# A group of low probabilities and half of h's low parts moved to GpSimd, odd heads' keys to ScalarE, one gate operation fewer

## The chip, the cores and the metric

The kernel runs on one core of a Trainium2 chip. The metric is the device time of one execution in microseconds, the median of several runs. An execution was also recorded by the hardware profiler; its rows are quoted below. Engines are named as the profile names them: PE is TensorE's matrix products and PEld its weight loads, DVE is VectorE, ACT is ScalarE, POOL is GpSimd, SP is the engine that issues the transfers.

## The reference

One gated block works on 32 rows of a batch. x has 256 tokens of 256 numbers in each row, the context y has 77 tokens of 192 numbers. There are 16 heads of 16 numbers, and 8 experts of which the best two count.

```python
# attention of the image tokens to the context, then a two-layer MLP
q, k, v = x_normed @ Wq + bq, y @ Wk + bk, y @ Wv + bv      # 16 heads of 16
attn = softmax(q k^T * scale)
h = relu((attn v) @ W1 + b1)
x = x + tanh(g_xattn) * (h @ W2 + b2)
# gated experts on the normed result
scores = maximum(x_normed2 @ gate_W + gate_b, 1e-4)
p = softmax(scores); keep the top 2, w = maximum(p, 0.1) over their sum
x = x + tanh(g_ffn) * sum_e w_e (x_normed2 @ expert_W[e] + expert_b[e]) / 2
```

## The kernel before

**High and low parts.** To keep fp32 accuracy with faster matrix products, most operands are split: a rounded high part (fp16 or fp32r) and a low part, which is the value less its high part. A product is then three products (low with high, high with low, high with high). ScalarE usually makes the high part out of PSUM, and VectorE or GpSimd the low part by a subtraction.

**Steps.** `run` calls `step(pair, u, s)` on every engine for s from 0 to 34. One step works on four rows of the batch at once, each at another stage: row b = s is in front (norm, keys, values, queries, row maxima), row m = s - 1 is in the middle (attention, MLP, second norm), row e = s - 2 is first with the experts (gate, products 0 to 4), and row f = s - 3 is last (products 5 to 7, store). Each engine has its own program, and the order of the calls in its `step` is the order of its work. Engines wait for each other by counting semaphores only. TensorE's order in a step is in `step` at line 965, VectorE's at 1354, ScalarE's at 641, GpSimd's at 446.

**Attention.** A row has eight groups of two heads. `exps` (ScalarE, L557 and L558) makes the exponentials of a group twice, as f32 `p_f` and as rounded `p_hi`; `p_low` makes `p_lo` as their difference on GpSimd (L373) or VectorE (L1182). `POOL_LOW` and `VECTOR_LOW` say which groups are whose: before, GpSimd has 1, 3, 4, 5, 6 and VectorE 0, 2, 7. `attend` on TensorE waits for the group's low part. The buffers hold four groups.

**The MLP.** `mlp_up` puts h into PSUM in two halves; `relus` (ScalarE, L603) writes each of four quarters twice, high part `h_hi` and f32 `h_f`; `h_low` (VectorE, L1277) subtracts them to `h_lo`; `mlp_down` (TensorE, L918) uses the quarters c = 0 to 3 in turn, with h's parts as weights that are loaded, and waits for the low part of each quarter the first time it needs it. `add_mlp` and the second norm follow on VectorE, with the scale of the norm on GpSimd (`second_norm_scale`), then `second_norm_transposes` on TensorE.

**Keys.** Sixteen stacked key blocks are transposed into one PSUM bank, `T_KEYS`. `kz_copy` copies the even heads' half on ScalarE (L611) and the odd heads' half on VectorE (L1252). The second half of the second MLP layer writes the same bank and waits for both copies.

**The gate.** Thirteen small operations on VectorE (`gate`, L1308), each behind the one before by the semaphore `gate_op`: scores with bias (`graw`), their maximum with 1e-4 (`gs`, L1323), the largest (`gm1`), the shifted scores (`gshift`) that ScalarE's `gate_exps` waits for (L639), differences of all pairs (`gdiff`, L1330), comparisons (`gbeat`, L1333), counts, sums, weights, `comb`. `stack_comb` on GpSimd waits for the last one.

**GpSimd's order in a step** is the low probabilities of row m, then key blocks (L427) of row b around `stack_comb`, the keys' low part, three additions for the experts' result, the queries' low part (L385), the values' two parts (L419, L421), the first norm's scale, the residual with its bias (`x_with_bias`, L366), and the second norm's scale (L358, L361).

## Time and profile before

| | |
|---|---|
| median of 3 runs | 1005.38 us |
| the runs | 1005.3, 1008.52, 1005.38 us |
| the profiled execution | 1003.91 us, span 1002.2 us |
| granted TensorE clock over the span | 0.977 of full speed |
| VectorE busy | 834.1 us in 2137 instructions |
| ScalarE busy | 732.1 us in 1517 instructions |
| GpSimd busy | 650.5 us in 856 instructions |

The span is the time from the first to the last instruction of the profiled execution. Matrix products are pipelined and their ends are modelled, so a following product can start before the one in front is shown as ended. A row of a timeline gives the start in us from the span's start, the length in us, the engine, the line of the kernel, the operation, what it writes and reads, and how many equal ones are merged; in brackets stands the idle time of the engine just before, and what ended it.

### The profile page before, as it was taken

How to read it: one execution, taken by the hardware profiler on the slowest of the kernel's cores; microseconds unless marked ns; L12 is line 12 of the kernel's file. 1: busy time of each engine (PE TensorE's matmuls, PEld its weight loads, DVE VectorE, ACT ScalarE, POOL GpSimd, SP SyncE). 2: the span in 40 equal slices, each digit the busy share in tenths (PEclk: the TensorE clock that was granted, in tenths of full speed). 3: DMA queues.
4: the chain of work that ended last, by engine and by line, in shares of the span. 5: the costliest groups of instructions: out<-in, count | busy, mean ns of one | idle time of the engine just before them, and what ended most of it. 6: DMA issues, size and time to landing. Idle time of an engine off the chain costs nothing.

```text
span 1002.2 us, 26189 instructions
## 1 busy us (share of the span) xinstructions
PE 941.7 (94%) x9410; PEld 668.3 (67%) x9410; DVE 834.1 (83%) x2137; ACT 732.1 (73%) x1517; POOL 650.5 (65%) x856
## 2 busy tenths in 40 slices
PE   3669999999999999999999999999999999999997
PEld 2446766766766776776777676677667766776753
DVE  5777888888888888888888889888888888888875
ACT  4756878777787877778787777778777877877661
POOL 5435766667776666776666677666677766666743
PEclk8589999999999999999999999999999999999999
DMA  6000000000000000000000000000000000000000
GB/s 196 27 14 11 15 14 25 25 25 22 26 14 15 25 26 25 23 23 17 15 25 25 25 23 14 26 15 25 25 25 22 15 17 23 25 12 12 12 13 22
DMA packets 17473, 24.62 MB, mean 25 GB/s; under 512 B 2799, under 2 KB 8897, under 8 KB 17345
## 3 DMA queue, kind: packets, MB, share of 16 engines
q1 hardware_dynamic: 17344, 22.94, 7.3%
q8 instruction: 77, 1.26, 0.5%
q14 instruction: 52, 0.42, 0.1%
HBM read 14.54 MB, written 8.39 MB: 23 GB/s over the span
## 4 chain that ended last, share of the span: by engine, by line
PE 56%; POOL 16%; DVE 9%; issue 9%; ACT 7%; DMA 1%; SPq 1%; POOLq 0%; DVEq 0%; ACTq 0%
PE e L735 19%; PE g L735 11%; PE t L918 9%; POOL k_block L427 8%; POOL p_lo L373 6%; PE t L784 4%; ACT p_hi L558 2%; PE g L935 2%; DVE stats L1086 2%; PE s L869 2%; DVE acc L1199 2%; PE s L804 1%; DVE kz L1252 1%; PE g L744 1%; DVE p_lo L1182 1%
## 5 line engine op out<-in xcount | busy, mean ns | idle before, releaser
L373 POOL TENSOR_TENSOR p_lo<-p_f,p_hi 77x512 f16<-77x512 f32 x160 | 183.4, 1162 | 227.6 <-ACT p_hi L558 227.6
L735 PE MATMUL e<-we_hi,x2T_lo 128*128 128x512 f16 x496 | 189.7, 382 | 4.8 <-DVE acc L1199 4.8
L735 PE MATMUL e<-we_hi,x2T_hi 128*128 128x512 f16 x496 | 188.9, 381 | 0.0
L735 PE MATMUL e<-we_lo,x2T_hi 128*128 128x512 f16 x496 | 188.9, 381 | 0.0
L557 ACT ACTIVATE p_f<-t 77x512 f32<-77x512 f32 x256 | 154.3, 603 | 24.2 <-PE t L784 23.8
L1199 DVE SCALAR_TENSOR_TENSOR acc<-e,comb,acc 128x256 f32<-128x256 f32 x307 | 146.0, 475 | 13.5 <-PE e L735 11.1
L558 ACT ACTIVATE p_hi<-t 77x512 f16<-77x512 f32 x256 | 154.4, 603 | 0.0
L1244 DVE TENSOR_REDUCE row_max<-s 128x6 f32<-128x462 f32 (+1 forms) x192 | 108.3, 578 | 32.1 <-PE s L869 32.0
L804 PEld LDWEIGHTS s<-v_hi,p_lo 77*128 77x128 f16 x1024 | 83.4, 96 | 38.3 <-issue 22.2
L804 PE MATMUL s<-v_hi,p_lo 77*128 77x17 f16 x1024 | 97.9, 172 | 11.0 <-DVE p_lo L1182 4.1
L806 PE MATMUL s<-v_hi,p_hi 77*128 77x17 f16 x1024 | 96.4, 170 | 0.0
L805 PE MATMUL s<-v_lo,p_hi 77*128 77x17 f16 x1024 | 96.3, 171 | 0.0
L427 POOL TENSOR_TENSOR k_block<-own_head,khT 128x616 f16<-128x616 f16 x64 | 93.6, 1464 | 4.1 <-ACT khT L588 4.1
L784 PE MATMUL t<-qsT,kz 128*77 128x256 f16 x512 | 90.6, 279 | 2.6 <-ACT p_hi L558 2.4
L735 PEld LDWEIGHTS e<-we_hi,x2T_hi 128*128 128x128 f16 x496 | 48.6, 98 | 59.2 <-issue 1.1
L603 ACT ACTIVATE h_hi<-g,b_cols,w_unscale 128x256 fp32r<-128x256 f32 x128 | 73.3, 572 | 19.8 <-PE g L735 19.8
L805 PEld LDWEIGHTS s<-v_lo,p_hi 77*128 77x128 f16 x1024 | 82.5, 97 | 7.3 <-issue 0.3
L806 PEld LDWEIGHTS s<-v_hi,p_hi 77*128 77x128 f16 x1024 | 81.6, 96 | 0.0
L615 ACT ACTIVATE qsT<-g 128x1024 f16<-128x1024 f16 x32 | 32.7, 1023 | 66.2 <-PE g L935 66.2
L735 PEld LDWEIGHTS e<-we_hi,x2T_lo 128*128 128x128 f16 x496 | 48.3, 97 | 48.1 <-DVE acc L1199 12.2
L1182 DVE TENSOR_TENSOR p_lo<-p_f,p_hi 77x512 f16<-77x512 f32 x96 | 73.7, 768 | 7.9 <-ACT p_hi L558 3.7
L918 PE MATMUL t<-w_hi,h_lo 128*128 128x256 f32 x256 | 77.3, 302 | 2.0 <-DVE h_lo L1277 1.4
(193 smaller groups left out, 2900.3 us busy)
## 6 DMA issues: line engine op xcount, KB each, us to landing
x_sb<-in_x SPq DMA_DIRECT2D x32, 256.0 KB, 2.6
out<-acc SPq DMA_DIRECT2D x32, 256.0 KB, 2.0
we_f<-in_L_ffn_expert_W SPq DMA_DIRECT2D x2, 1024.0 KB, 11.0
y_sb<-in_ctx SPq DMA_DIRECT2D x32, 57.8 KB
w_f<-in_L_xattn_W SPq DMA_DIRECT2D x2, 512.0 KB, 7.3
wq_f<-in_L_xattn_Wq SPq DMA_DIRECT2D x1, 256.0 KB, 3.9
wkv_f<-in_L_xattn_Wk SPq DMA_DIRECT2D x1, 192.0 KB, 3.1
wkv_f<-in_L_xattn_Wv SPq DMA_DIRECT2D x1, 192.0 KB, 3.9
```

Of the source, the lines that this page charges most:

```text
L373: pool.tensor_tensor(p_lo[:, r].rearrange("m h n -> m (h n)"), p_f[:, r, :], p_hi[:, r].rearrange("m h n -> m (h n)"), ALU.subtract).then_ ...
L427: pool.tensor_tensor(k_block[:, c * PAIRS:(c + 1) * PAIRS, :], own_head[:], khT[:, c, :].unsqueeze(1).to_broadcast([P, PAIRS, M]), ALU.mul ...
L557: act.activation(p_f[:, r, :], TT[g % 2][0:M, :], ACT.Exp, scale=SCALE).then_inc(exps_done, 1)
L558: act.activation(p_hi[:, r].rearrange("m h n -> m (h n)"), TT[g % 2][0:M, :], ACT.Exp, scale=SCALE).then_inc(exps_done, 1)
L735: mm = pe.matmul(out_ap, a, c, start=(i == 0), stop=(i == n - 1))
L784: mm = pe.matmul(TT[g % 2][0:M, e * N:(e + 1) * N], kz[:, g, e, :], qsT[:, g, :], start=True, stop=True)
L804: pe.matmul(dst, lo, v_hi[:, u, h, :], start=True, stop=False)
L805: pe.matmul(dst, hi, v_lo[:, u, h, :], start=False, stop=False)
L806: mm = pe.matmul(dst, hi, v_hi[:, u, h, :], start=False, stop=True)
L918: mm = pe.matmul(T_DOWN[t][:, 0:D], a[:, c, rows], w[:, c, :], start=(c == 0 and i == 0), stop=(c == HC - 1 and i == 2))
L1199: dve.scalar_tensor_tensor(out=acc[:, u, t, :], in0=BANK[product_banks(r)[i]][:, j * D:(j + 1) * D], scalar=comb[:, u, t, 2 * c + j:2 * c ...
L1244: dve.tensor_reduce(row_max[:, t, h:h + n], S[i % 2][:, 0:n * M].rearrange("p (h m) -> p h m", h=n), AX.X, ALU.max).then_inc(max_taken, 1)
```

## The change

- `POOL_LOW` is (1, 2, 3, 4, 5, 6) and `VECTOR_LOW` (0, 7): group 2's low probabilities are made by GpSimd.
- `h_low` of quarters 1 and 3 runs on GpSimd, quarters 0 and 2 stay on VectorE. The semaphore `h_lo_done` becomes two, `h_lo_vector` and `h_lo_pool`. On GpSimd quarter 1 stands behind `q_low` and ahead of `v_parts`, quarter 3 behind `v_parts`.
- `kz_copy` on VectorE is gone; ScalarE copies both halves, one behind the other.
- The gate has 12 operations. `graw` has a ninth column that holds 1e-4, so the largest can be taken of the raw scores, and the maximum with 1e-4 is made together with the subtraction of the largest. The comparisons use the shifted scores. One more memset fills the ninth column once.
- On GpSimd `x_with_bias` moves behind the second norm's scale.

```diff
-CONSTS = EARLY + 1 + 7
+CONSTS = EARLY + 1 + 8
-POOL_LOW = (1, 3, 4, 5, 6)
-VECTOR_LOW = (0, 2, 7)
+POOL_LOW = (1, 2, 3, 4, 5, 6)
+VECTOR_LOW = (0, 7)
-GATE_OPS = 13
+GATE_OPS = 12
...
+            def h_low(b, c):
+                pool.wait_ge(relu_done, 8 * b + 2 * c + 2)
+                at_least(pool, mlp_in_psum, 2 * b)
+                pool.tensor_tensor(h_lo[:, c, :], h_f[:, c, :], h_hi[:, c, :].bitcast(F32), ALU.subtract).then_inc(h_lo_pool, 1)
...
+            pool.memset(graw[:, :, E:E + 1], EPS).then_inc(consts_ready, 1)
...
                 if has(s, 0):
                     q_low(b)
+                if has(s, -1):
+                    h_low(m, 1)
+                if has(s, 0):
                     v_parts(b, u)
+                if has(s, -1):
+                    h_low(m, 3)
...
                 if has(s, 1) and s > 0:
                     first_norm_scale(n)
-                if has(s, 1):
-                    x_with_bias(n, nu)
                 if has(s, -1):
                     second_norm_scale(m, 0)
                     second_norm_scale(m, 1)
+                if has(s, 1):
+                    x_with_bias(n, nu)
...
-                act.activation(kz[0:SLOT, :, 0, :], src[0:SLOT], ACT.Copy).then_inc(kz_done, 1)
+                for i in range(2):
+                    rows = slice(i * SLOT, (i + 1) * SLOT)
+                    act.activation(kz[rows, :, i, :], src[rows], ACT.Copy).then_inc(kz_done, 1)
...
-                            pe.wait_ge(h_lo_done, 4 * b + c + 1)
+                            pe.wait_ge((h_lo_vector, h_lo_pool)[c % 2], 2 * b + c // 2 + 1)
...
                 elif k == 2:
-                    ins = dve.tensor_scalar(gs[:], graw[:], EPS, None, ALU.max)
+                    ins = dve.tensor_reduce(gm1[:], graw[:], AX.X, ALU.max)
                 elif k == 3:
-                    ins = dve.tensor_reduce(gm1[:], gs[:], AX.X, ALU.max)
+                    ins = dve.scalar_tensor_tensor(out=gshift[:], in0=graw[:, :, 0:E], scalar=EPS, in1=wide(gm1),
+                                                   op0=ALU.max, op1=ALU.subtract)
...
-                if mid:
-                    p_low(m, 2)
...
                 if front:
                     take_max(b, 1)
                     take_max(b, 2)
-                    kz_copy(b)
...
                 if mid:
                     h_low(m, 0)
-                    h_low(m, 1)
                 if first:
                     add_expert(e_pair, e, eu, 1, 0, s - 2)
                 if mid:
                     h_low(m, 2)
                 if first:
                     add_expert(e_pair, e, eu, 1, 1, s - 2)
-                if mid:
-                    h_low(m, 3)
```

## Rows read from the trace of the kernel before

**Rows 1.** The page, part 1: busy us, share of the span, instructions.
```profile
PE 941.7 (94%) x9410; PEld 668.3 (67%) x9410; DVE 834.1 (83%) x2137; ACT 732.1 (73%) x1517; POOL 650.5 (65%) x856
```

**Rows 2.** The chain of work in order of time: start us, us, what.
```profile
505.23 2.90 PE t L918 x24
...
510.85 1.02 ACT qsT L619
...
534.61 2.90 PE t L918 x24
```

**Rows 3.** Instructions of single lines: count, ns min/median/max, first and last start us, form.
```profile
L1277 DVE TENSOR_TENSOR h_lo<-h_f,h_hi x128: 393/463/1329, 60.5 to 974.9; 128x256 fp32r<-128x256 f32 x128
L1182 DVE TENSOR_TENSOR p_lo<-p_f,p_hi x96: 677/689/4465, 36.6 to 964.2; 77x512 f16<-77x512 f32 x96
L421 POOL TENSOR_TENSOR v_lo<-kv,v_hi x32: 651/712/719, 21.6 to 945.0; 77x256 f16<-77x256 f32 x32
L413 POOL TENSOR_TENSOR acc<-acc,bias_sum x32: 1259/1268/1275, 119.3 to 998.5; 128x512 f32<-128x512 f32 x32
```

**Rows 4.** TensorE's timeline in the second half of a step.
```profile
503.63 0.39 PE L735 MATMUL e<-we_hi,x2T_lo 128*128 128x512 f16 x1 [0.17 <-DVE acc L1199]
...
506.14 0.32 PE L918 MATMUL t<-w_hi,h_lo 128*128 128x256 f32 x1
...
511.47 0.60 PE L945 MATMUL g<-ident,xn 128*128 128x128 f32 x4
```

**Rows 5.** ScalarE's timeline, same stretch: key copy, first and last ReLU.
```profile
500.55 0.68 ACT L611 ACTIVATE kz<-t 64x616 f16<-64x616 f16 x1
501.80 0.56 ACT L603 ACTIVATE h_hi<-g,b_cols,w_unscale 128x256 fp32r<-128x256 f32 x1 [0.57 <-PE g L735]
...
504.95 0.60 ACT L603 ACTIVATE h_f<-g,b_cols,w_unscale 128x256 f32<-128x256 f32 x1
```

**Rows 6.** VectorE's timeline, same stretch.
```profile
500.71 0.48 DVE L1252 COPY kz<-t 64x616 f16<-64x616 f16 x1
...
505.59 0.43 DVE L1277 TENSOR_TENSOR h_lo<-h_f,h_hi 128x256 fp32r<-128x256 f32 x1
```

**Rows 7.** Timeline of TensorE's weight loads, same stretch.
```profile
506.07 0.19 PEld L918 LDWEIGHTS t<-w_hi,h_lo 128*128 128x128 f32 x1
```

**Rows 8.** VectorE's timeline, gate, first half of the step.
```profile
486.80 0.56 DVE L1323 TENSOR_SCALAR gs<-graw 128x16 f32<-128x16 f32 x1
...
488.61 0.29 DVE L1333 TENSOR_TENSOR gbeat<-gdiff,beat_from 128x128 f32<-128x128 f32 x1
...
489.14 0.68 DVE L1207 TENSOR_TENSOR kv<-g,bkv_rows 77x512 f32<-77x512 f32 x1
```

**Rows 9.** GpSimd's timeline, same stretch as rows 8.
```profile
486.17 1.16 POOL L373 TENSOR_TENSOR p_lo<-p_f,p_hi 77x512 f16<-77x512 f32 x1 [4.68 <-ACT p_hi L558]
489.06 2.29 POOL L373 TENSOR_TENSOR p_lo<-p_f,p_hi 77x512 f16<-77x512 f32 x2 [1.74 <-ACT p_hi L558]
```

**Rows 10.** ScalarE's timeline, same stretch as rows 8.
```profile
487.81 0.22 ACT L639 ACTIVATE gexp<-gshift 128x16 f32<-128x16 f32 x1 [0.57 <-DVE gshift L1327]
...
489.86 0.41 ACT L565 ACTIVATE k_hi<-kv 77x256 f16<-77x256 f32 x1
490.87 0.59 ACT L557 ACTIVATE p_f<-t 77x512 f32<-77x512 f32 x1 [0.60 <-PE t L784]
```

**Rows 11.** GpSimd's timeline in the second half of the step.
```profile
502.50 1.16 POOL L385 TENSOR_TENSOR q_stack<-q,q_hi 128x512 f16<-128x512 f32 x1
...
504.28 0.71 POOL L421 TENSOR_TENSOR v_lo<-kv,v_hi 77x256 f16<-77x256 f32 x1
...
506.22 1.29 POOL L366 TENSOR_TENSOR xb<-x_sb,b2g_rows 128x512 f32<-128x512 f32 x1
```

**Rows 12.** Timelines of GpSimd and VectorE, second norm, end of the step.
```profile
510.30 0.55 POOL L361 TENSOR_TENSOR rstd<-ve,minus_half 128x1 f32<-128x1 f32 x1
...
510.89 0.41 DVE L1297 TENSOR_SCALAR xn<-x,mv,rstd 128x256 f32<-128x256 f32 x1 [0.71 <-POOL rstd L361]
```

More of the change, by code:

```diff
@@ L147, in gated_block @@
         x2T_hi, x2T_lo = sb("x2T_hi", [P, 2, KC, N], F16), sb("x2T_lo", [P, 2, KC, N], F16)
-        graw, gs, gshift, gexp, gcount, gfloor, gw = (
-            sb(n, [P, T, E]) for n in ("graw", "gs", "gshift", "gexp", "gcount", "gfloor", "gw"))
+        graw = sb("graw", [P, T, E + 1])
+        gshift, gexp, gcount, gfloor, gw = (
+            sb(n, [P, T, E]) for n in ("gshift", "gexp", "gcount", "gfloor", "gw"))
         gdiff, gbeat = sb("gdiff", [P, T, E, E]), sb("gbeat", [P, T, E, E])
@@ L208, in gated_block @@
         h_in_psum, relu_done = sem("h_in_psum"), sem("relu_done")
-        h_lo_done = sem("h_lo_done")
+        h_lo_vector, h_lo_pool = sem("h_lo_vector"), sem("h_lo_pool")
         mlp_in_psum, x1_done = sem("mlp_in_psum"), sem("x1_done")
@@ L598, in relus @@
                 act.wait_ge(h_in_psum, 2 * b + c + 1)
-                at_least(act, h_lo_done, 4 * b)
+                at_least(act, h_lo_vector, 2 * b)
+                at_least(act, h_lo_pool, 2 * b)
                 at_least(act, mlp_in_psum, 2 * b)
@@ L637, in gate_exps @@
             def gate_exps(b):
-                act.wait_ge(gate_op, GATE_OPS * b + 4)
+                act.wait_ge(gate_op, GATE_OPS * b + 3)
                 act.activation(gexp[:], gshift[:], ACT.Exp).then_inc(gate_exp, 1)
@@ L1245, in take_max @@
                                   AX.X, ALU.max).then_inc(max_taken, 1)
-            def kz_copy(b):
-                dve.wait_ge(kz_in_psum, b + 1)
-                at_least(dve, scores_ready, 8 * b)
-                src = T_KEYS[:].bitcast(F16)[:, 0:PAIRS * MP].rearrange("p (j m) -> p j m", j=PAIRS)[:, :, 0:M]
-                dve.tensor_copy(kz[SLOT:2 * SLOT, :, 1, :], src[SLOT:2 * SLOT]).then_inc(kz_done, 1)
             def stack_max(b):
@@ L1276, in h_low @@
                     at_least(dve, mlp_in_psum, 2 * b)
-                dve.tensor_tensor(h_lo[:, c, :], h_f[:, c, :], h_hi[:, c, :].bitcast(F32), ALU.subtract).then_inc(h_lo_done, 1)
+                dve.tensor_tensor(h_lo[:, c, :], h_f[:, c, :], h_hi[:, c, :].bitcast(F32), ALU.subtract).then_inc(h_lo_vector, 1)
             def add_mlp(b, u, t):
@@ L1311, in gate @@
                     dve.wait_ge(gate_in_psum, b + 1)
-                elif k == 8:
+                elif k == 7:
                     dve.wait_ge(gate_exp, b + 1)
@@ L1318, in gate @@
                 if k == 1:
-                    ins = dve.scalar_tensor_tensor(out=graw[:], in0=G_GATE[:, 0:T * E].rearrange("p (t e) -> p t e", t=T),
+                    ins = dve.scalar_tensor_tensor(out=graw[:, :, 0:E], in0=G_GATE[:, 0:T * E].rearrange("p (t e) -> p t e", t=T),
                                                    scalar=w_unscale[:, 1:2], in1=gb_rows[:].unsqueeze(1).to_broadcast([P, T, E]),
@@ L1329, in gate @@
                 elif k == 5:
-                    ins = dve.tensor_tensor(gdiff[:], gs[:].unsqueeze(2).to_broadcast([P, T, E, E]),
-                                            gs[:].unsqueeze(3).to_broadcast([P, T, E, E]), ALU.subtract)
+                    ins = dve.tensor_tensor(gbeat[:], gdiff[:], beat_from[:], ALU.is_gt)
                 elif k == 6:
-                    ins = dve.tensor_tensor(gbeat[:], gdiff[:], beat_from[:], ALU.is_gt)
+                    ins = dve.tensor_reduce(gcount[:], gbeat[:], AX.X, ALU.add)
@@ L1334, in gate @@
                 elif k == 7:
-                    ins = dve.tensor_reduce(gcount[:], gbeat[:], AX.X, ALU.add)
+                    ins = dve.tensor_reduce(gsum[:], gexp[:], AX.X, ALU.add)
                 elif k == 8:
-                    ins = dve.tensor_reduce(gsum[:], gexp[:], AX.X, ALU.add)
-                elif k == 9:
                     ins = dve.scalar_tensor_tensor(out=gfloor[:], in0=wide(gsum), scalar=W_THRES, in1=gexp[:],
                                                    op0=ALU.mult, op1=ALU.max)
-                elif k == 10:
+                elif k == 9:
@@ L1343, in gate @@
                     ins = dve.scalar_tensor_tensor(out=gw[:], in0=gcount[:], scalar=TOP_K - 0.5, in1=gfloor[:],
                                                    op0=ALU.is_lt, op1=ALU.mult)
+                elif k == 10:
+                    ins = dve.tensor_reduce(gtot[:], gw[:], AX.X, ALU.add)
                 elif k == 11:
-                    ins = dve.tensor_reduce(gtot[:], gw[:], AX.X, ALU.add)
-                elif k == 12:
                     ins = dve.reciprocal(grt[:], gtot[:])
@@ L1377, in step @@
                     gate(e, eu, 3)
+                if first:
                     gate(e, eu, 4)
-                if mid:
-                    p_low(m, 2)
-                if first:
                     gate(e, eu, 5)
                     gate(e, eu, 6)
-                    gate(e, eu, 7)
                 if front:
@@ L1389, in step @@
                 if first:
+                    gate(e, eu, 7)
                     gate(e, eu, 8)
-                    gate(e, eu, 9)
                 if front:
@@ L1394, in step @@
                 if first:
-                    gate(e, eu, 10)
+                    gate(e, eu, 9)
                 if front:
@@ L1406, in step @@
                 if first:
-                    gate(e, eu, 11)
+                    gate(e, eu, 10)
                 if last:
@@ L1410, in step @@
                 if first:
-                    gate(e, eu, 12)
+                    gate(e, eu, 11)
                 if last:
@@ L1414, in step @@
                 if first:
-                    gate(e, eu, 13)
+                    gate(e, eu, 12)
                 if last:
```

3 lines of the change are left out of this document (2 added, 1 removed).

## The prediction

> **What bounds the kernel now.** I read the page's busy times first. TensorE is busy 94% of the span and VectorE 83%, GpSimd 65% [rows 1]; no engine is so full that its sum alone sets the time, so the order of the waits inside a step decides. The chain in order of time comes next. It repeats every 534.61 - 505.23 = 29.38 us from one second MLP layer to the next [rows 2], so a step is a closed loop, and what is added to that loop in one step is added in every step. The low parts of h run from 60.5 to 974.9 us, four to a row of the batch, 32 rows: 31 steps of 29.5 us [rows 3]. I count 30 of them for the sum, since the first ones still wait for weights.
>
> Then I followed one step through the timelines, where the change's tiles meet this loop. At 503.63 TensorE starts expert product 2 after waiting 0.17 us for VectorE's additions [rows 4]. That wait looks like what the lighter VectorE would remove, but it is not alone. ScalarE's eight ReLUs start at 501.80, when TensorE has the first half of h ready (0.57 us idle before), follow each other every (504.95 - 501.80)/7 = 0.45 us, and the last ends at 504.95 + 0.60 = 505.55 [rows 5]. VectorE makes the last low part of h at once, 505.59 to 506.02 [rows 6]; TensorE loads it as weights at 506.07 [rows 7] and starts that product at 506.14, whose 0.32 us is the longer one of that layer [rows 4]. So two paths end at the last quarter of the second layer at nearly the same time: TensorE's own, and h in PSUM, ReLUs, low part 3. Neither can be shortened alone with effect. Everything behind is tight: the layer, expert 3 and the query transposes on TensorE, then ScalarE's query copies (510.85 on the chain) [rows 2].
>
> **The change, part by part.**
>
> *VectorE.* It loses a group of low probabilities (0.69), two low parts of h (2 x 0.46) [rows 3], the key copy (0.48) [rows 6] and the gate's maximum with the constant (0.56) [rows 8]: 2.65 us of 29.38. In the second half of the step the key copy stands ahead of the additions that TensorE waits for at 503.63, so that wait of 0.17 goes, up to the 0.17 us and no more on this path. What is late next is low part 3 of h, which hangs on the ReLUs and not on VectorE's load. I therefore cost this gain at nothing.
>
> *ScalarE* gets the second key copy, as large as its own, 0.68 us at 500.55 [rows 5]. Back to back the two end about 501.9 less the overlap of some 0.1 us that successive ReLUs show (0.57 long, 0.45 apart). ReLUs wait for TensorE until 501.80, so the copy fills the 0.57 us idle. Cover gone, it costs up to 0.1 us a step; taken as 0.
>
> *GpSimd, the group.* Group 2 runs right behind group 1: group 1 starts at 486.17 and lasts 1.16 [rows 9], ScalarE has finished group 2's exponentials at 487.81 - 0.57 = 487.24 [rows 10], so group 2 takes about 487.31 to 488.46, in the gap ahead of 489.06 where GpSimd waits for ScalarE [rows 9]. On its own queue it costs nothing.
>
> *GpSimd, h's low parts 1 and 3.* This is the term that counts. Low part 1 needs the fourth ReLU (501.80 + 3 x 0.45 + 0.57 = 503.72) and GpSimd, which ends the queries' low part at 502.50 + 1.16 = 503.66 [rows 11]: start 503.79. The length of such an operation on GpSimd has no row. The nearest: 256 columns into f16 take 0.65 undisturbed, 512 columns into f32 1.27 [rows 3], 512 into f16 1.16 [rows 9]. The extra for f32 at half the columns is (1.27 - 1.16)/2 = 0.055, so 0.70. It ends at 504.49, long before TensorE wants it. Then the values' two operations stand in the queue, which took 503.66 to 504.28 + 0.71 = 504.99, so 1.33 us, with two of VectorE's low parts in their way [rows 11]. With one in the way I take about 1.1: low part 3 can start at 505.6, as the last ReLU has ended (505.55, with 0.07 to GpSimd, as from 487.24 to 487.31). Start 505.62, end 506.32, against 506.02 for VectorE now: **+0.30** a step; a release to TensorE of about the same length adds 0.01: +0.31. TensorE is there by 506.14 - 0.17, so it waits, and layer 2, expert 3 and all behind move by that much.
>
> Bounds: the least is a start at 505.55 and 0.65 us, 506.20, +0.18; a gain is excluded, as the ReLU ends at 505.55 and no row of this size on GpSimd is under 0.65. The most is the full 1.33 for the values (505.82) and 0.75, 506.57, +0.55. I take 0.31, by the ReLU, because the values' operations have less in their way than now.
>
> The Trainium skill, GPSIMD Engine Reference, "Performance versus the Vector engine", says that a two-input elementwise operation is 1.96 times as long on GpSimd as on VectorE (measured there at 2048 columns). By that the 0.43 us would be 0.84, an estimate from that page, low part 3 would end at 506.46 and the time would be about 1018.9. The groups here show 1.16 against 0.69, 1.68 times [rows 3, 9], and the sum goes by those rows.
>
> *The gate.* The removed maximum lasted 0.56 us for 16 columns and ended at 487.36, just behind the group on GpSimd at 487.33 [rows 8, 9]: it was held by it. The new third operation reads two tensors of SBUF and will be held in the same place, so the shifted scores are ready at about 487.37, the gate's exponential at 487.41 and not 487.81 [rows 10]. ScalarE gains 0.40 there and hands it back: it next waits for TensorE's scores, as at 490.87 (0.60 idle) [rows 10]. Gain on the loop 0.
>
> *The order on GpSimd.* The residual with bias (1.29 us) moves from 506.22 [rows 11] to behind the second norm's scale (510.30 to 510.85) [rows 12]. It is wanted a step later, so as work it is hidden. But it starts just as VectorE's second normalisation (510.89, 0.41) [rows 12] wants to start, and may hold it as the gate's operation is held: until 512.1 plus the lateness. TensorE's transposes of it run from 511.47 [rows 4], their second half about 511.77, later by 0.31 in this forecast, 512.08; so 0 to 0.25 us of wait. The chain there runs through ScalarE's query copies [rows 2], which cover some of it; I take 0, upper bound 0.25.
>
> *Start.* One more small memset, once: below 1 us, taken as 0.
>
> Sum: 0.31 x 30 = 9.3 us. The profiled execution is 1003.91 (span 1002.2 and 1.7 around it): 1013.2. The median of the runs shown is 1.5 above it, so 1005.38 + 9.3 = **1014.7**.
>
> **The rivals.**
>
> *GpSimd holds the gate.* Moving group 2 to GpSimd fills the stretch in which VectorE's comparison (two SBUF inputs) ran undisturbed, 0.29 us at 488.61 [rows 8]. Differences would be held by group 2 until about 488.46 and end near 488.62, the comparison wants to start near 488.66; group 3 wants to start 1.25 us after the gate's exponential (489.06 - 487.81 [rows 9, 10]), at 487.41 + 1.25 = 488.66. That is a tie. If group 3 comes first, the comparison ends at about 489.96, the keys' and values' sum starts 0.24 later (489.14 is 0.53 after 488.61, 0.29 of it the comparison [rows 8]) at 490.20 and not 489.14, the key's high part at 490.92 and not 489.86, and since that stands ahead of group 5's exponential on ScalarE, group 5 starts at 490.92 + 0.41 less the overlap of 0.1 = 491.23 and not 490.87 [rows 10]: +0.36 a step, in series with the 0.31. Time 1014.7 + 10.8 = 1025.5. For it: the held operation of 0.56 us. Against it: the tie may fall the other way, or step by step. The Trainium skill, SBUF — State Buffer, "Who interferes with whom", states that a VectorE instruction with two SBUF inputs and a GpSimd instruction that reads SBUF exclude each other for the whole instruction, first come first; by that rule this rival's time stands if group 3 is first. The held 0.56 us agrees with it.
>
> *The second normalisation waits for the moved residual*, uncovered: up to 0.25 x 30 = 7.5 more, 1022.
>
> *Faster.* Low part 3 doesn't decide, and TensorE's wait of 0.17 at expert 2 was the real bound: 0.17 x 30 = 5.1 less, 1000.3. That holds if low part 3 is ready by about 505.85, before 506.02; it would need ReLUs that end earlier. Against it stands the ReLUs' end at 505.55; for it, only that the product at 506.14 starts nearly on its beat.
>
> *No difference.* Low part 3 ends near 506.1: 1005 to 1008.
>
> **How the numbers follow.** Forecast 0.48 (its own bounds 1010.8 to 1021.9, the least and the most of the low part times 30); GpSimd ahead in the gate 0.25; the moved residual uncovered 0.07; no difference 0.09; faster 0.11. A difference under 0.3% (3 us) is about what a measurement of this kernel can't tell from none. So slower 0.80, same 0.09, faster 0.11. The range takes the three slower cases with their bounds: from 1008 (a little under the least of +0.18, 5.4 us) to 1028 (the gate rival and some more).
>
> **What would show it.** Right: TensorE waits for GpSimd's low part of h in nearly every step, the second layer's last quarter 0.3 us later against the ReLUs, a period near 29.7, no wait for VectorE at expert 2. GpSimd's low part about 0.70 us, starting just behind the last ReLU. The gate rival shows as a comparison over 1 us long and a key copy on ScalarE a microsecond later. The residual shows as a second normalisation of 1.2 us. I am wrong if the low part takes 0.4 us on GpSimd, or if the loop turns out to run past the ReLUs, so that the period falls below 29.38.

## The result, and the profile after

The changed kernel takes 1058.67 us (median of 4 runs, 1058.17 to 1058.97) against 1005.51 for the kernel before: a ratio of 1.0519 [1.0502, 1.0537]. It is slower, as forecast, but by 53 us and not by 9.3, and the time lies above the range. A step, from one low part 3 of h on GpSimd (501.19) to the next (532.39), lasts 31.20 us; before it was 29.38 [rows 2]. 1.8 us over 30 steps are 54 us, about the 53 measured.

The page's first part, against [rows 1]:

```profile
PE 949.7 (90%) x9410; PEld 677.6 (64%) x9410; DVE 853.7 (81%) x1977; ACT 761.6 (72%) x1549; POOL 725.4 (69%) x953
```

VectorE has 160 instructions less. By the prediction's list it lost 2.65 us of work a step, some 85 us in 32 steps, and yet its busy time rose from 834.1 to 853.7. So its remaining instructions became longer, by about 105 us in all. Which ones, the instructions of single lines show (count, ns min/median/max):

```profile
L1337 DVE TENSOR_TENSOR gdiff<-gshift x32: 292/1242/1245, 74.8 to 1038.1; 128x128 f32<-128x128 f32 x32
L1340 DVE TENSOR_TENSOR gbeat<-gdiff,beat_from x32: 293/1296/1309, 76.1 to 1038.5; 128x128 f32<-128x128 f32 x32
L419 POOL TENSOR_TENSOR h_lo<-h_f,h_hi x64: 721/724/736, 60.6 to 1029.5; 128x256 fp32r<-128x256 f32 x64
```

The differences in the kernel before:

```profile
L1330 DVE TENSOR_TENSOR gdiff<-gs x32: 276/281/292, 75.5 to 983.5; 128x128 f32<-128x128 f32 x32
```

The gate's differences and comparisons, 0.28 and 0.29 us each in the kernel before (the comparison in [rows 8]), take 1.24 and 1.30 with the same shapes. VectorE's timeline of one step (start us, us):

```profile
506.33 1.35 DVE L1305 TENSOR_SCALAR xn<-x,mv,rstd 128x256 f32<-128x256 f32 x1 [0.71 <-POOL rstd L362]
...
512.67 1.25 DVE L1337 TENSOR_TENSOR gdiff<-gshift 128x128 f32<-128x128 f32 x1
513.95 1.29 DVE L1340 TENSOR_TENSOR gbeat<-gdiff,beat_from 128x128 f32<-128x128 f32 x1
...
515.48 0.68 DVE L1222 TENSOR_TENSOR kv<-g,bkv_rows 77x512 f32<-77x512 f32 x1
...
519.67 2.08 DVE L1197 TENSOR_TENSOR p_lo<-p_f,p_hi 77x512 f16<-77x512 f32 x1
```

GpSimd's timeline of the same step:

```profile
501.19 0.73 POOL L419 TENSOR_TENSOR h_lo<-h_f,h_hi 128x256 fp32r<-128x256 f32 x1
...
506.26 1.27 POOL L367 TENSOR_TENSOR xb<-x_sb,b2g_rows 128x512 f32<-128x512 f32 x1
511.45 2.32 POOL L374 TENSOR_TENSOR p_lo<-p_f,p_hi 77x512 f16<-77x512 f32 x2 [3.91 <-ACT p_hi L570]
513.93 1.17 POOL L374 TENSOR_TENSOR p_lo<-p_f,p_hi 77x512 f16<-77x512 f32 x1 [0.16 <-ACT p_hi L570]
...
517.65 2.27 POOL L374 TENSOR_TENSOR p_lo<-p_f,p_hi 77x512 f16<-77x512 f32 x2 [1.18 <-ACT p_hi L570]
519.89 1.25 POOL L433 TENSOR_TENSOR k_block<-own_head,khT 128x616 f16<-128x616 f16 x1
```

Read the two beside each other. Groups 1 and 2 end at 511.45 + 2.32 = 513.77, and the differences, begun at 512.67, end at 513.92. Group 3 starts at 513.93, two hundredths before the comparison (513.95), and ends at 515.10; the comparison ends at 515.24. The moved residual ends at 507.53, the second normalisation beside it at 507.68. And group 7's low part, VectorE's, is begun at 519.67 while group 6 still runs to 519.92; then key block 0 runs to 521.14, and the low part ends at 521.75. In each pair VectorE's instruction ends 0.14 to 0.6 us after GpSimd's, wherever it began. A VectorE instruction that is longer than its like elsewhere, and ends so behind one of GpSimd, is called held below.

ScalarE's timeline: the last ReLU of one step, then the key's high part with the wait in front of it and group 5's exponential (before: [rows 10]), both key copies as one row and the first ReLU (before: [rows 5]).

```profile
500.51 0.60 ACT L616 ACTIVATE h_f<-g,b_cols,w_unscale 128x256 f32<-128x256 f32 x1
...
516.19 0.42 ACT L577 ACTIVATE k_hi<-kv 77x256 f16<-77x256 f32 x1 [0.95 <-DVE kv L1222]
516.52 0.58 ACT L569 ACTIVATE p_f<-t 77x512 f32<-77x512 f32 x1
...
527.14 1.38 ACT L626 ACTIVATE kz<-t 64x616 f16<-64x616 f16 x2
528.55 0.57 ACT L616 ACTIVATE h_hi<-g,b_cols,w_unscale 128x256 fp32r<-128x256 f32 x1
```

TensorE's timeline after: the last quarter of the second layer, group 7, expert product 1, the first product of the MLP.

```profile
501.97 0.38 PE L933 MATMUL t<-w_hi,h_lo 128*128 128x256 f32 x1 [0.59 <-POOL h_lo L419]
...
521.81 0.18 PE L819 MATMUL s<-v_hi,p_lo 77*128 77x17 f16 x1 [1.13 <-DVE p_lo L1197]
...
524.90 0.39 PE L750 MATMUL e<-we_hi,x2T_lo 128*128 128x512 f16 x1 [0.27 <-DVE acc L1214]
...
526.88 0.28 PE L750 MATMUL g<-oT_hi,w_lo 128*128 128x256 f16 x1
```

And two of the same rows of TensorE before:

```profile
498.31 0.39 PE L735 MATMUL e<-we_hi,x2T_lo 128*128 128x512 f16 x1
...
500.28 0.28 PE L735 MATMUL g<-oT_hi,w_lo 128*128 128x256 f16 x1
```

With these points a step can be cut into pieces that join end to end, so the differences add up to the longer step:

| from, to | before | after | longer | what is late |
|---|---|---|---|---|
| last quarter of layer 2, group 5's exponential | 14.12 | 14.55 | 0.43 | the keys' sum, behind the held gate |
| to expert product 1 | 7.44 | 8.38 | 0.94 | group 7's low part, held by key block 0 |
| to the first product of the MLP | 1.97 | 1.98 | 0.01 | |
| to the first ReLU | 1.52 | 1.67 | 0.15 | the second key copy on ScalarE |
| to the last quarter of layer 2 | 4.34 | 4.62 | 0.28 | low part 3 of h on GpSimd |
| sum | 29.39 | 31.20 | 1.81 | |

(14.12 is 490.87 + 29.385 - 506.14, where 29.385 is the mean of the four steps from a first ReLU at 384.26 to the one at 501.80; 14.55 is 516.52 - 501.97; 4.62 is 501.97 + 31.20 - 528.55; the others are differences of two rows.) TensorE's waits name the second and the last of them (us in total, times, longest):

```profile
PE s L819 <- DVE p_lo L1197: 36.4, 34, 3.1
PE t L933 <- POOL h_lo L419: 19.4, 33, 0.6
```

In the kernel before, group 7 was already close to this. There VectorE and GpSimd had:

```profile
494.05 0.80 DVE L1182 TENSOR_TENSOR p_lo<-p_f,p_hi 77x512 f16<-77x512 f32 x1
```

```profile
492.03 2.28 POOL L373 TENSOR_TENSOR p_lo<-p_f,p_hi 77x512 f16<-77x512 f32 x2 [0.68 <-ACT p_hi L558]
494.27 1.70 POOL L427 TENSOR_TENSOR k_block<-own_head,khT 128x616 f16<-128x616 f16 x1
```

Low part 7 was held only to the end of group 6 (494.31), went next, and key block 0 was the one that took longer, 1.70 instead of 1.25. In the changed kernel that order is the other way round.

### The profile page after: what moved, and what is told of

The parts are those of the page before. It is cut to its first block, busy times and chain, and to the rows that moved or that the text cites. A ratio compares the mean times of both kernels' runs of the same rounds, so it can differ in the third digit from the quotient of the medians.

```text
span 1057.1 us, 26251 instructions
## 1 busy us (share of the span) xinstructions
PE 949.7 (90%) x9410; PEld 677.6 (64%) x9410; DVE 853.7 (81%) x1977; ACT 761.6 (72%) x1549; POOL 725.4 (69%) x953
## 4 chain that ended last, share of the span: by engine, by line
POOL 36%; ACT 18%; issue 16%; PE 16%; DVE 13%; POOLq 0%; DMA 0%; ACTq 0%; DVEq 0%
POOL k_block L433 7%; PE t L933 6%; POOL p_lo L374 6%; PE e L750 5%; ACT p_hi L570 5%; POOL h_lo L419 4%; ACT p_f L569 4%; DVE gbeat L1340 4%; POOL bias_sum L408 3%; DVE gdiff L1337 3%; POOL q_stack L386 3%; POOL bias_sum L406 3%; ACT qsT L634 3%; POOL v_lo L427 2%; POOL comb_hi L395 2%
## 5 line engine op out<-in xcount | busy, mean ns | idle before, releaser
L374 POOL TENSOR_TENSOR p_lo<-p_f,p_hi 77x512 f16<-77x512 f32 x192 | 222.2, 1165 | 179.1 <-ACT p_hi L570 179.1
L819 PE MATMUL s<-v_hi,p_lo 77*128 77x17 f16 x1024 | 101.0, 172 | 43.9 <-DVE p_lo L1197 36.4
L821 PE MATMUL s<-v_hi,p_hi 77*128 77x17 f16 x1024 | 99.1, 170 | 0.0
L820 PE MATMUL s<-v_lo,p_hi 77*128 77x17 f16 x1024 | 99.0, 171 | 0.0
L933 PE MATMUL t<-w_hi,h_lo 128*128 128x256 f32 x256 | 80.1, 313 | 19.4 <-POOL h_lo L419 19.4
L1197 DVE TENSOR_TENSOR p_lo<-p_f,p_hi 77x512 f16<-77x512 f32 x64 | 88.9, 1389 | 8.3 <-ACT p_hi L570 4.2
L433 POOL TENSOR_TENSOR k_block<-own_head,khT 128x616 f16<-128x616 f16 x64 | 80.8, 1264 | 4.0 <-ACT khT L600 4.0
L419 POOL TENSOR_TENSOR h_lo<-h_f,h_hi 128x256 fp32r<-128x256 f32 x64 | 46.4, 724 | 51.6 <-ACT h_f L616 51.6
L607 ACT ACTIVATE oT_hi<-g 128x512 f16<-128x512 f32 x32 | 19.1, 597 | 86.6 <-PE g L895 86.6
```

The lines of the kernel that those rows point to most:

```text
L374: pool.tensor_tensor(p_lo[:, r].rearrange("m h n -> m (h n)"), p_f[:, r, :], p_hi[:, r].rearrange("m h n -> m (h n)"), ALU.subtract).then_ ...
L433: pool.tensor_tensor(k_block[:, c * PAIRS:(c + 1) * PAIRS, :], own_head[:], khT[:, c, :].unsqueeze(1).to_broadcast([P, PAIRS, M]), ALU.mul ...
L819: pe.matmul(dst, lo, v_hi[:, u, h, :], start=True, stop=False)
L820: pe.matmul(dst, hi, v_lo[:, u, h, :], start=False, stop=False)
L821: mm = pe.matmul(dst, hi, v_hi[:, u, h, :], start=False, stop=True)
L933: mm = pe.matmul(T_DOWN[t][:, 0:D], a[:, c, rows], w[:, c, :], start=(c == 0 and i == 0), stop=(c == HC - 1 and i == 2))
```

## The experiments

Theory A: the loss comes mostly from GpSimd's instructions that hold VectorE's beside them, first of all the moved group 2, which holds the gate and through it shifts group 7. Theory B, the forecast: the loss comes from the low part of h on GpSimd, with group 2 free. A third possibility is that GpSimd is simply too full. Ratios are to the kernel before on the same chip, with a 95% interval.

### Each part taken back, or made alone

**Group 2 back on VectorE**, all else as changed:

```diff
-POOL_LOW = (1, 2, 3, 4, 5, 6)
-VECTOR_LOW = (0, 7)
+POOL_LOW = (1, 3, 4, 5, 6)
+VECTOR_LOW = (0, 2, 7)
...
+                if mid:
+                    p_low(m, 2)
```

> Changed kernel, but group 2's low probabilities are again made by VectorE. Theory A (group 2 on GpSimd holds VectorE's gate operations, the keys' sum waits behind them, and the last group's low part comes so late that GpSimd's key block gets ahead of it): the step loses 0.37 + 0.94 us of its 31.20, so about 41 us go and the time is about 1018. Theory B (the low parts of h on GpSimd, for which TensorE waits 0.6 us in every step, and GpSimd's load carry the loss): a group less on GpSimd gives little, above 1045.

1020.34 us, 1.0142 [1.0127, 1.0158]. 38 of the 53 us are gone with this one group. TensorE's wait for group 7's low part falls from 36.4 to 4.1 us, and that for h's low part stays (19.1).

**Group 2 alone**, the kernel before with only that group moved (the same diff, the other way round):

> Kernel before, with group 2's low probabilities moved to GpSimd and nothing else changed. Theory A: the gate's differences and comparison become 1.2 to 1.3 us long, the attention's last group waits about 1 us for its low part, and the time is about 1005 + 1.3 x 30 = 1045. Theory B: 1005, within 5 us.

1062.88 us, 1.0564 [1.0547, 1.0580]: by itself it costs a little more than the whole change, and 18 us more than theory A had named. VectorE's rows for low part 3 of h and for the shifted scores, GpSimd's for the residual, and ScalarE's for the gate's exponential that waits for the shifted scores:

```profile
503.92 1.23 DVE L1277 TENSOR_TENSOR h_lo<-h_f,h_hi 128x256 fp32r<-128x256 f32 x1
...
516.12 0.92 DVE L1327 TENSOR_TENSOR gshift<-gs,gm 128x16 f32<-128x16 f32 x1
```

```profile
503.58 1.29 POOL L366 TENSOR_TENSOR xb<-x_sb,b2g_rows 128x512 f32<-128x512 f32 x1
```

```profile
517.07 0.22 ACT L639 ACTIVATE gexp<-gshift 128x16 f32<-128x16 f32 x1 [1.31 <-DVE gshift L1327]
```

With the old gate another operation meets group 2: the subtraction of 16 columns, 0.17 us before, takes 0.92, ScalarE waits 1.31 us, while differences and comparison, which theory A had named, keep their 0.29. Which instruction is held differs between the two gates; in both of them one of the chain is. And a second thing is added here that the changed kernel doesn't have: GpSimd comes to the residual 3.45 us after the first ReLU (500.13) instead of 4.42, so low part 3 of h, which VectorE still makes, takes 1.23 us beside it instead of 0.43, and TensorE waits 17.6 us for it in 30 steps. So the 56 us of this run are not the price of group 2 inside the change.

**All of h's low parts back on VectorE**, group 2 still on GpSimd (the lines that go are GpSimd's):

```diff
-                if has(s, -1):
-                    h_low(m, 1)
...
-                if has(s, -1):
-                    h_low(m, 3)
...
                 if mid:
                     h_low(m, 0)
+                    h_low(m, 1)
...
+                if mid:
+                    h_low(m, 3)
```

> Changed kernel, but all four low parts of h are again made by VectorE. Theory A: only the 0.28 us from the first ReLU to the last quarter of the second layer go, 0.28 x 30 = 8 us, so about 1050. Theory B: most of the loss goes, below 1025.

1049.80 us, 1.0436 [1.0419, 1.0454]: 8.9 us less than the changed kernel. This is the term on which theory B rested, and it has about the size forecast, but it is a sixth of the loss.

**Group 2 and h's low parts back**, the first and the third of these diffs together:

> Changed kernel with group 2 and all low parts of h back on VectorE; both key copies on ScalarE, the 12-operation gate and the moved residual stay. Against 1020 with group 2 back alone. Theory A (low part 3 of h ends 0.3 us later on GpSimd, and the second key copy delays the ReLUs by 0.15 us): 0.3 x 30 = 9 us less, about 1011. If the low parts cost nothing: 1020.

1012.89 us, 1.0069 [1.0052, 1.0086]: 7.5 us less than with group 2 back alone.

**Group 2 and the key copy back**, the first diff and this one:

```diff
-                for i in range(2):
-                    rows = slice(i * SLOT, (i + 1) * SLOT)
-                    act.activation(kz[rows, :, i, :], src[rows], ACT.Copy).then_inc(kz_done, 1)
+                act.activation(kz[0:SLOT, :, 0, :], src[0:SLOT], ACT.Copy).then_inc(kz_done, 1)
...
+                    kz_copy(b)
```

> Changed kernel with group 2 and the odd heads' key copy back on VectorE; h's low parts 1 and 3 stay on GpSimd. Theory A: the ReLUs start 0.15 us earlier against TensorE's first layer, 4.5 us less than 1020, about 1016. If the second copy on ScalarE fits its idle time, as I had forecast: 1020.

1017.07 us, 1.0117 [1.0098, 1.0136]: 3.3 us less than with group 2 back alone.

**Group 2, h's low parts and the key copy back**, all of these diffs, so that the gate of 12 operations and the later residual are left:

> Changed kernel with group 2, h's low parts and the key copy all back on VectorE: what is left of the change is the 12-operation gate and the residual moved behind the second norm's scale. Theory A: both cost and give nothing on the loop, 1005 to 1007, as before. If the second normalisation, held by the moved residual for 1 us, is uncovered: up to 1012.

1008.27 us, 1.0023 [1.0015, 1.0032], a little above the 1005 to 1007 expected. Here too one instruction of VectorE is held, the second normalisation, by the residual:

```profile
512.12 1.35 DVE L1300 TENSOR_SCALAR xn<-x,mv,rstd 128x256 f32<-128x256 f32 x1 [0.70 <-POOL rstd L362]
```

**The gate alone**, 12 operations in the kernel before:

```diff
-GATE_OPS = 13
+GATE_OPS = 12
...
-                    ins = dve.tensor_scalar(gs[:], graw[:], EPS, None, ALU.max)
+                    ins = dve.tensor_reduce(gm1[:], graw[:], AX.X, ALU.max)
```

> Changed kernel with everything undone but the 12-operation gate: the residual is back ahead of the second norm's scale too. Against 1008.3 with the residual moved. If the moved residual holds VectorE's second normalisation, and that is what is left: 1005.6, as before. If the shorter gate is what costs: 1008. If the gate's gain of 0.4 us for ScalarE reaches the loop: below 1000.

1007.50 us, 1.0009 [0.9997, 1.0021]: no difference that can be measured.

One after the other the parts come to: group 2 38.3 us (1058.67 - 1020.34), h's low parts 7.5 (to 1012.89), the key copy 4.6 (to 1008.27), the residual with the gate 2.7 (to 1005.6 for the kernel before). By the ratios, each of which compares on one chip, they are 37.9, 7.3, 4.6 and 2.3 us. The last one does not lie in the steps: from the third on, the steps of that run's trace last 29.38 us, as before, in spite of the held normalisation. The 3.4 us by which its profiled span is longer (1005.6 against 1002.2) lie in the first two steps (62.86 us from the first ReLU of the first row to that of the third, against 61.07) and behind the first ReLU of the last row (32.9 against 31.1). What makes these longer was not tried.

### Is it the hold, and not the work?

**Low parts of group 2 wait until the gate's comparison is done.** GpSimd does the same work as in the changed kernel, later:

```diff
                     for g in POOL_LOW:
+                        if g == 2 and has(s, -2):
+                            pool.wait_ge(gate_op, GATE_OPS * e + 5)
                         p_low(m, g)
```

> Changed kernel, but GpSimd waits for the gate's comparison ahead of group 2; the work of both engines is that of the changed kernel. If the loss is that GpSimd's groups 2 and 3 hold the differences and the comparison: both fall to 0.3 us, the key sum is in time, the last group isn't held, and the time is that with group 2 back on VectorE, 1018 to 1022. If it is GpSimd's added work: 1059 or more, as a wait can only make GpSimd later.

1022.27 us, 1.0143 [1.0124, 1.0162]. An added wait makes the kernel 36 us faster than the changed one, just above the 1018 to 1022 of theory A. Single lines:

```profile
L1339 DVE TENSOR_TENSOR gdiff<-gshift x32: 291/292/293, 77.1 to 1002.6; 128x128 f32<-128x128 f32 x32
L1342 DVE TENSOR_TENSOR gbeat<-gdiff,beat_from x32: 291/293/294, 77.4 to 1002.9; 128x128 f32<-128x128 f32 x32
```

Both operations have their 0.29 us in all 32 steps, and in VectorE's timeline group 7's low part is back at 0.80:

```profile
504.75 0.80 DVE L1199 TENSOR_TENSOR p_lo<-p_f,p_hi 77x512 f16<-77x512 f32 x1
```

This settles it between A and the third possibility: GpSimd is as full as in the changed kernel (busy 720.0 us against 725.4), and the loss of group 2 is gone. The first two late places of the table go together here: with the gate undisturbed, group 7 falls the right way as well. That the one follows from the other is likely, but this run moves both.

**The two consequences apart.** First, the keys' sum ahead of the gate's differences, so that a held gate can't delay the keys:

```diff
+                if front:
+                    kv_with_bias(b)
                 if first:
                     gate(e, eu, 4)
...
-                if front:
-                    kv_with_bias(b)
```

> Changed kernel, but on VectorE the sum of keys and values stands ahead of the gate's differences, comparison and count, so it isn't queued behind operations that GpSimd holds. Theory A: the wait for the keys' high part (0.37 us a step) goes, about 1047, and more, down to 1019, if the last group's low part comes earlier too. Theory B: no difference from the changed kernel, 1059.

1056.72 us, 1.0504 [1.0489, 1.0520], hardly better, where theory A had 1047 or less; by the time alone the run would speak for B. VectorE's timeline, and then a wait of TensorE:

```profile
513.54 0.69 DVE L1222 TENSOR_TENSOR kv<-g,bkv_rows 77x512 f32<-77x512 f32 x1 [0.98 <-PE g L750]
...
517.28 1.38 DVE L1234 CAST q_hi<-q 128x512 f16<-128x512 f32 x1
...
520.63 0.84 DVE L1197 TENSOR_TENSOR p_lo<-p_f,p_hi 77x512 f16<-77x512 f32 x1
```

```profile
PE g L865 <- DVE q_hi L1234: 19.7, 30, 1.2
```

The keys were in time, as meant, and group 7 was not held for long either. But now group 5's low part meets the cast of the queries, 0.41 us before and 1.38 here, and TensorE waits for that in 30 steps. Group 7's low part, behind the cast in VectorE's order, starts 4.56 us after group 5's exponential (516.07) instead of 3.15. The hold moved to another instruction.

Second, the small copies of `stack_comb` ahead of key block 0, so that behind group 6 the long key block isn't next:

```diff
                     for g in POOL_LOW:
                         p_low(m, g)
-                if has(s, 0):
-                    key_blocks(b, 0)
                 if has(s, -2):
                     stack_comb(e, eu)
                 if has(s, 0):
+                    key_blocks(b, 0)
                     key_blocks(b, 1)
```

> Changed kernel, but on GpSimd the four small operations that stack the gate's weights stand ahead of the first key block, so that this block isn't queued right behind group 6 while VectorE's last group (group 7) waits. Theory A1 (the last group's low part is held by the first key block for a whole block, which costs 0.94 us of the step): its 2.08 us fall below 1 us, TensorE's wait of 1.13 us for it goes, and the time is about 1058.7 - 0.94 x 30 = 1030. Theory A2 (the last group is late because VectorE itself is late behind the held gate): the wait stays, and the time is above 1050.

1033.84 us, 1.0277 [1.0259, 1.0295]. VectorE's timeline:

```profile
502.27 1.23 DVE L1336 TENSOR_TENSOR gdiff<-gshift 128x128 f32<-128x128 f32 x1
503.53 1.30 DVE L1339 TENSOR_TENSOR gbeat<-gdiff,beat_from 128x128 f32<-128x128 f32 x1
...
509.26 0.80 DVE L1196 TENSOR_TENSOR p_lo<-p_f,p_hi 77x512 f16<-77x512 f32 x1
```

The gate is held as in the changed kernel, group 7 is not, and 24.8 us of the loss are gone: 0.83 a step, of the 0.94 in the table. What is left of group 2's 38 us, 13.5 or 0.45 a step, is the 0.43 of the gate.

The table's pieces, worked out in the same way as means of four or five steps of each run's trace, show where each of these runs differs (the piece between expert product 1 and the MLP's first product is 1.97 or 1.98 in all):

| piece that ends at | before | changed | group 2 back | GpSimd waits | keys' sum first | small copies first | group 2 alone |
|---|---|---|---|---|---|---|---|
| group 5's exponential | 14.11 | 14.55 | 14.17 | 14.18 | 14.18 | 14.55 | 14.19 |
| expert product 1 | 7.44 | 8.38 | 7.44 | 7.44 | 8.63 | 7.48 | 8.64 |
| the first ReLU | 1.52 | 1.67 | 1.67 | 1.67 | 1.67 | 1.68 | 1.52 |
| the last quarter of layer 2 | 4.34 | 4.62 | 4.61 | 4.62 | 4.61 | 4.61 | 5.06 |

With group 2 back on VectorE, or made to wait, both places that are put down to it are gone but for 0.06 of the first; with the small copies first only the second is gone, and with the keys' sum first the first is gone and the second has grown. The places that are put down to the key copy and to h's low parts stay as long as those do. In "group 2 alone" nearly all of the loss is group 7's (1.20 a step) and that of the low part held by the residual (0.72).

### A version that might beat both

If the two paths that meet at the last quarter of the second layer decide, TensorE should take the products that don't need h's low part first, and VectorE should come to its low parts free of the statistics that stand in front of expert 0's second addition. All five kernels here are made from the kernel before.

**Order of the products:**

```diff
-                            pe.wait_ge(h_lo_done, 4 * b + c + 1)
-                            pe.wait_ge(relu_done, 8 * b + 2 * c + 2)
-                        for i, (a, w) in enumerate(((h_lo, w2_hi), (h_hi, w2_lo), (h_hi, w2_hi))):
+                            pe.wait_ge(relu_done, 8 * b + 2 * c + 1)
+                        for i, (a, w) in enumerate(((h_hi, w2_lo), (h_hi, w2_hi), (h_lo, w2_hi))):
+                            if t == 0 and i == 2:
+                                pe.wait_ge(h_lo_done, 4 * b + c + 1)
```

> Kernel before, but the second layer takes the two products of h's high part first and the product of its low part last, in every quarter, and waits for the low part only there. If two paths end at the last quarter together (low part 3, and TensorE's own path through the wait at expert 2), taking slack on one alone gives next to nothing: 1004 to 1006. If low part 3 alone is the bound: 0.24 us a step, 998.

1004.93 us, 0.9984 [0.9973, 0.9995]: the only version below the kernel before, by 0.16%, half of the 0.3% that the prediction names as the least to be told from no change.

**The same, with the first norm's statistics behind expert 0's additions:**

```diff
-                if has(s, 1) and s > 0:
-                    first_norm_stats(n_pair, n, nu)
...
+                    add_expert(e_pair, e, eu, 0, 1, s - 2)
...
+                    first_norm_stats(n_pair, n, nu)
...
-                if first:
-                    add_expert(e_pair, e, eu, 0, 1, s - 2)
```

> The same, and on VectorE the statistics of the first norm (0.75 us) stand behind both additions of expert product 0, so that TensorE's wait at expert 2 goes too. If two paths end there together, both are now shorter by 0.17 to 0.28 us: 997 to 1000. If neither is on the loop: 1005.

1042.41 us, 1.0365 [1.0349, 1.0381], where a gain was expected. VectorE, GpSimd and a wait of TensorE:

```profile
522.81 1.40 DVE L1278 TENSOR_TENSOR h_lo<-h_f,h_hi 128x256 fp32r<-128x256 f32 x2
...
525.28 1.44 DVE L1278 TENSOR_TENSOR h_lo<-h_f,h_hi 128x256 fp32r<-128x256 f32 x1
```

```profile
523.22 0.71 POOL L421 TENSOR_TENSOR v_lo<-kv,v_hi 77x256 f16<-77x256 f32 x1
...
525.16 1.27 POOL L366 TENSOR_TENSOR xb<-x_sb,b2g_rows 128x512 f32<-128x512 f32 x1
```

```profile
PE t L919 <- DVE h_lo L1278: 34.0, 32, 1.1
```

Low part 3 wants to start 0.12 us behind the residual and takes 1.44 instead of 0.43. Before, it was the residual that came later (506.22 against 505.59) [rows 6, 11].

**The same with the gate of 12 operations**, as in the diff of the gate alone:

> The same two edits on the kernel with the 12-operation gate. If the shorter gate gives nothing on the loop: the same as with 13 operations, 997 to 1000.

1043.18 us, 1.0373 [1.0356, 1.0390]: the same hold (TensorE waits 33.9 us for low parts of h), the gate changes nothing.

**The same as the second, and GpSimd's residual waits for the last low part of h:**

```diff
                 if has(s, 1):
+                    if has(s, -1):
+                        pool.wait_ge(h_lo_done, 4 * m + 4)
                     x_with_bias(n, nu)
```

> order_stats, but GpSimd starts the residual only when VectorE has made low part 3. If that part was held by the residual (1.44 us where 0.43 is its length), it is made in 0.43 us, and what both shorter paths give is seen: 0.2 to 0.28 us a step less than before, 998 to 1001. If order_stats lost its time elsewhere: 1035 or more.

1015.11 us, 1.0078 [1.0063, 1.0093]. 27 us come back, but there is no gain, where 998 to 1001 was expected. VectorE and GpSimd:

```profile
510.61 1.40 DVE L1280 TENSOR_TENSOR h_lo<-h_f,h_hi 128x256 fp32r<-128x256 f32 x2
...
513.07 0.41 DVE L1280 TENSOR_TENSOR h_lo<-h_f,h_hi 128x256 fp32r<-128x256 f32 x1
```

```profile
511.02 0.71 POOL L421 TENSOR_TENSOR v_lo<-kv,v_hi 77x256 f16<-77x256 f32 x1
```

Low part 3 is free, but low parts 0 and 1 now take 1.40 together, since the values' low part is in front of low part 1. In the version with the order alone these were:

```profile
505.53 1.00 DVE L1278 TENSOR_TENSOR h_lo<-h_f,h_hi 128x256 fp32r<-128x256 f32 x2
```

```profile
506.33 0.71 POOL L421 TENSOR_TENSOR v_lo<-kv,v_hi 77x256 f16<-77x256 f32 x1
```

The statistics, moved right in front of the low parts, make low part 0 start 1.90 us after the first ReLU (508.71) and not 1.69 (503.84). Low part 1, which would follow some 0.4 later, then comes when the values' low part runs already. Low part 3 starts at 513.07, 0.6 after the last ReLU's end (511.87 + 0.60).

**The same as the second, with the residual behind the second norm's scale** (the move of the change):

```diff
-                if has(s, 1):
-                    x_with_bias(n, nu)
                 if has(s, -1):
                     second_norm_scale(m, 0)
                     second_norm_scale(m, 1)
+                if has(s, 1):
+                    x_with_bias(n, nu)
```

> order_stats with the residual behind the second norm's scale, as the change has it. Low part 3 isn't held, but the second normalisation is, which cost 0.1 us a step with everything else undone: 3 us more than with the wait, 1001 to 1004. If order_stats lost its time elsewhere: 1035 or more.

1021.40 us, 1.0140 [1.0125, 1.0155], where 1001 to 1004 was expected. Low parts 0 and 1 take 1.43 for the same reason, and the second normalisation 1.35, held by the residual. ScalarE's first ReLU and first query copy here:

```profile
513.55 0.56 ACT L603 ACTIVATE h_hi<-g,b_cols,w_unscale 128x256 fp32r<-128x256 f32 x1 [0.57 <-PE g L735]
...
522.02 1.02 ACT L615 ACTIVATE qsT<-g 128x1024 f16<-128x1024 f16 x1 [2.39 <-PE g L936]
```

They are 8.47 us apart, against 8.09 with the order alone (503.84 to 511.93); and the period, from one gate's exponential to the next (499.56 to 529.44), is 29.88 against 29.35 (ScalarE's attention copies, 499.70 to 529.05). 0.53 x 30 is 16 us, the measured difference 16.5. The other 0.15 of the 0.53 lies behind the query copy, where TensorE now waits for the held second normalisation in 31 steps (12.9 us in all). That the statistics' move would gain anything once no low part is held was not shown.

## Where the prediction was right and where it failed

**What bounds the kernel.** The reading held: a closed loop, in which 0.43 us at the keys costs 0.43 us a step. That two paths end at the last quarter together fits: making the one through low part 3 later by 0.28 us costs 0.28 a step, and letting TensorE take that low part last (order of the products) gave only 0.16%. That the other path is the one through the additions at 503.63 was not shown. The product of 0.32 us at 506.14 is no sign of it: it is not the longest of its layer, whose first one, at 504.96, has 0.38.

**h's low parts: right.** Forecast 0.70 us, measured 0.724; start 0.07 after the last ReLU forecast, 0.08 measured (501.19 against 500.51 + 0.60); +0.31 a step forecast, +0.28 in the table; 9.3 us forecast, 7.5 and 8.9 by taking it back. TensorE waits 0.59 for it. On the price of moving such an operation the Trainium skill, GPSIMD Engine Reference, "Performance versus the Vector engine", has 1.96 times, at 2048 columns; here 0.724 against VectorE's 0.43 is 1.68 times, and the measurement decides.

**The key copy: a term mis-sized.** Forecast 0, bound 0.1 a step; it costs 0.15, by taking it back 3.3 to 4.6 us. The cover of 0.57 us was there. But the overlap of 0.1 that the ReLUs show does not hold for the two copies: 0.68 each, 1.38 for both, and the ReLU behind them starts only when they have ended (528.55 against 527.14 + 1.38 = 528.52).

**Group 2: the step that failed.** The direction came out right, but the term on which the forecast rested is a sixth of the loss. "On its own queue it costs nothing" is true of GpSimd's queue and was the wrong question. It costs 38 us through VectorE. The prediction had the mechanism as a rival with a chance of 0.25: differences held by group 2, group 3 against the comparison as a tie at 488.66, the keys late by 0.36 a step. The rows show each of these: differences of 1.25 us, group 3 0.02 ahead of the comparison, group 5 later by 0.43. The likeliest case was to be the forecast without this rival, and the reason given against it, that the tie may fall the other way, was no more than the tie itself. With group 2 alone, where another operation of the gate meets it, the gate's chain is held all the same.

**What no case had.** The larger half of group 2's loss, 0.83 to 0.94 a step, is the second tie, group 7 against key block 0. Its rows stood in the trace of before (0.80 and 1.70, shown above), both longer than the same operations undisturbed. The prediction followed the rival as far as group 5 and stopped there. So even the rival's 1025.5 was short by about 33 us: 28 for group 7 and 4.6 for the key copy make most of it.

**The residual: 0, as forecast.** The second normalisation is held (1.35 us; 1.2 was named), and with everything else undone the steps are no longer than before (29.38); the bound was 7.5. By the prediction's own terms that bound is too low: 512.1 + 0.31 is 0.33 behind the 512.08 at which the transposes want it, and not 0.25. What the prediction did not see is the other side of this move: at its old place the residual comes within reach of low part 3 of h as soon as GpSimd runs ahead, which costs 0.72 us a step with group 2 alone.

**The gate: 0, as forecast.** 1.0009 [0.9997, 1.0021].

**VectorE's relief: 0, as forecast**, though for more than the reason given. TensorE's wait for the additions did not go but moved to expert product 1 and grew to 0.27. **Faster** and **no difference** are out.

The Trainium skill, SBUF — State Buffer, "Who interferes with whom", has a rule that fits all of this: an instruction of VectorE with two inputs in SBUF and one of GpSimd that reads SBUF shut each other out for a whole instruction. The gate's two operations agree (0.29 against 1.25 and 1.29). It also names casts and operations with a scalar among those that can be shut out, in some modes; the cast of 1.38 and the normalisation of 1.35 us agree. The prediction cites the rule on two inputs and says that the held 0.56 us agree with it; but that operation, the maximum with a constant [rows 8], has one input and a scalar, so it goes with the second sort.

## What to carry to other kernels

An instruction moved to GpSimd can be paid for on VectorE as well: list which of VectorE's instructions run in the stretch that it will fill, and who waits for them, before counting the free time of GpSimd's own queue. A VectorE instruction that is longer than the same shape elsewhere in the trace may already be in such a meeting, so look at what GpSimd runs beside it; the busy share hides it, since the time held counts as busy. Where two such instructions start within a few hundredths of each other, an edit far away can turn their order round, and a wait that keeps GpSimd off the critical stretch can be worth more than the work it delays.

## What the runs showed of the hardware

- **The end of a held instruction.** Differences ended 0.15 us after group 2, the comparison 0.14 after group 3, the second normalisation 0.15 after the residual. A longer one (512 columns, low part 7) ended 0.6 after the key block.
- **Who goes first when both wait is not settled.** When group 6 ended, low part 7 had been waiting for 0.2 to 0.3 us in both kernels. Key block 0 went first where its keys had been ready 0.22 us before that end (519.70 against 519.92), and second where they had been ready for 0.12 (494.19 against 494.31); with group 2 back on VectorE and with the added wait, at 0.11 and 0.12, it went second too. But with the small copies in that place, ready for a microsecond, the low part went first. No run tests this by itself.
- **Two copies on ScalarE without overlap.** They read and write different partitions (0 to 63, 64 to 127), whereas the ReLUs that overlap use all 128. Whether that is the cause was not tried.
